# A recommendation tower on one core: ids loads, the split of a product over two steps, the last block's copies, and four products of ones at the start

## The reference

```python
x = layer_norm(dense_t @ Wd.T, gd, bd)                       # 512 x 128
y = layer_norm(jnp.einsum('bnd,ed->bne', sparse_t, Ws), gs, bs)
y = jnp.einsum('bne,pn->bep', y, Wsi)
y = jnp.swapaxes(layer_norm(y, gsi, bsi), 1, 2)              # 512 x 32 x 128
T = jnp.concatenate([x[:, None, :], y], axis=1)              # 512 x 33 x 128
Z = jnp.einsum('bnd,bmd->bnm', T, T)
out = layer_norm(Z[:, TRIL_I, TRIL_J] @ Wl.T, gl, bl) * mask # the first 384 kept
h = jnp.concatenate([out, r_dense_t], axis=1)
h = jnp.maximum(h @ W_top1 + b_top1, 0.0)
h = jnp.maximum(h @ W_top2 + b_top2, 0.0)
y = h @ W_top3
```

## Time and profile before

| | |
|---|---|
| median of 3 executions | 299.44 us (298.72 to 300.36) |
| profiled execution | 297.24 us, span 295.4 us |
| TensorE matmuls busy | 154.6 us, 52% |
| VectorE busy | 130.5 us, 44% |
| ScalarE busy | 107.0 us, 36% |
| GpSimd busy | 100.9 us, 34% |
| granted TensorE clock, whole span | 0.763 |

### The profile page before, as it was taken

One profiled execution on the slowest core, in us unless ns is written; L12 is line 12 of the kernel. 1 busy time (PEld: TensorE's weight loads), 2 busy tenths in 40 slices (PEclk: granted clock), 3 DMA queues, 4 the chain that ended last, 5 costly groups with the idle time before them and its releaser, 6 DMA issues.

```text
span 295.4 us, 4646 instructions
## 1 busy us (share of the span) xinstructions
PE 154.6 (52%) x1819; PEld 116.9 (40%) x1819; DVE 130.5 (44%) x296; ACT 107.0 (36%) x242; POOL 100.9 (34%) x111
## 2 busy tenths in 40 slices
PE   0736400026000400022069797769898998898797
PEld 0514300003000300002015485447776777776696
DVE  4852300000100600000065778458989789978533
ACT  2020100000100100000046766587777767776522
POOL 3777777777777777773000000000000000000100
PEclk9997765555755555555559967579999999999999
DMA  6352231111111111110000000200002000100000
GB/s 192 105 203 63 97 98 25 25 26 27 27 27 27 27 27 27 26 25 18 0 0 3 0 2 0 46 0 2 3 3 46 0 2 2 39 11 23 23 2 0
DMA packets 6259, 9.59 MB, mean 32 GB/s; under 512 B 2687, under 2 KB 3794, under 8 KB 6110
## 3 DMA queue, kind: packets, MB, share of 16 engines
q0 software_dynamic: 3392, 3.45, 6.0%
q1 hardware_dynamic: 2488, 5.08, 5.7%
q10 hardware_dynamic: 358, 0.77, 0.9%
HBM read 8.01 MB, written 0.00 MB: 27 GB/s over the span
## 4 chain that ended last, share of the span: by engine, by line
issue 43%; PE 31%; ACT 13%; DVE 8%; DMA 3%; SPq 1%; ACTq 0%; DVEq 0%
PE psB L307 7%; ACT Zs L595 6%; PE psU L295 4%; PE psG L280 3%; PE psW L338 3%; DVE B L768 2%; ACT U L561 2%; DMA small_sb<-in_small 2%; DVE qA L746 2%; DVE prod L739 2%; PE psH L443 2%; PE psZ L322 2%; ACT sdB L573 2%; PE psW L443 1%; PE psH L452 1%
## 5 line engine op out<-in xcount | busy, mean ns | idle before, releaser
L253 POOL DMA_INDIRECT g_sb<-in_table,row_id x104 | 99.4, 956 | 31.7 <-issue 31.4
L768 DVE TENSOR_TENSOR B<-psB,bias 128x512 f32<-128x512 f32 x32 | 20.8, 687 | 114.2 <-remote 47.5
L307 PE MATMUL psB<-U,ws_g 64*128 64x512 f32 x64 | 21.9, 765 | 63.5 <-issue 52.9
L210 POOL DMA_DIRECT2D Zt<-Zs x2 | 1.1, 552 | 141.4 <-ACT Zs L595 141.4
L295 PE MATMUL psU<-wsi_x,g_sb 128*128 128x192 f32 (+4 forms) x128 | 26.6, 362 | 34.6 <-issue 30.0
L295 PEld LDWEIGHTS psU<-wsi_x,g_sb 128*128 128x128 f32 x128 | 24.1, 232 | 39.4 <-issue 33.3
L595 ACT ACTIVATE Zs<-psZ 32x264 f32<-32x264 f32 x60 | 37.1, 618 | 1.3 <-PE psZ L322 0.2
L567 ACT ACTIVATE sqB<-B 128x512 f32<-128x512 f32 x32 | 19.7, 633 | 43.2 <-DVE B L768 43.2
L307 PEld LDWEIGHTS psB<-U,ws_g 64*128 64x128 f32 x64 | 5.6, 215 | 68.1 <-issue 53.7
L280 PEld LDWEIGHTS psG<-gram,sT 128*128 128x128 f32 x104 | 15.8, 230 | 32.3 <-issue 24.0
L280 PE MATMUL psG<-gram,sT 128*128 128x128 f32 x104 | 19.3, 334 | 17.6 <-issue 17.6
(11 more groups left out here) (132 smaller groups left out, 217.8 us busy)
## 6 DMA issues: line engine op xcount, KB each, us to landing
g_sb<-in_table,row_id POOLq DMA_INDIRECT x104
wl_sb<-in_wl SPq DMA_DIRECT2D x1, 1280.0 KB
w_sb<-in_w SPq DMA_DIRECT2D x2, 512.0 KB
w_sb<-in_w SPq DMA_DIRECT2D x1, 768.0 KB
small_sb<-in_small SPq DMA_DIRECT2D x1, 615.5 KB, 6.4
dense_sb<-in_dense ACTq DMA_DIRECT2D x1, 512.0 KB, 3.6
Zt<-Zs SPq DMA_DIRECT2D x3, 80.0 KB
Zt<-Zs SPq DMA_DIRECT2D x3, 70.0 KB
```

Source lines behind the costliest of these rows:

```text
L253: pool.indirect_dma_start(g_sb[:, k, h * DSP:(h + 1) * DSP], None, table, bass.IndirectOffsetOnAxis(row_id[:, 2 * k + h:2 * k + h + 1], 0) ...
L307: pe.matmul(psB[h][:, :], ws_g[h * DSP:(h + 1) * DSP, :], U[h * DSP:(h + 1) * DSP, u % 2, :], start=True, stop=True).then_inc(B_done, 1)
L768: dve.tensor_tensor(B[:, h, :].rearrange("p (s j) -> p s j", j=PROJ), psB[h][:, :].rearrange("p (s j) -> p s j", j=PROJ), bias[:, :].rearr ...
```

## The change

The ids go to SBUF as one flat tile, so that each of the two loads is one contiguous run in each partition. The second ids load moves behind that of `small_sb` on SP's queue, and ScalarE's queue waits until the first ids have landed before it issues the load of `dense_sb`. TensorE multiplies a matrix of ones by itself four times (128x512 each, into `psU`) before it waits for `small_sb`; the `fills` thresholds of others go from 4 to 5.

`EARLY` goes from 12 to 6. `output(b-1)` moves from ahead of `project` to behind `inner`, and writes `psH` in place of `psW`; VectorE's copy of it moves behind `sums_a`. Waits follow the new places. For the third block (`LAST - 1`) `squares_w` moves behind ScalarE's last DMAs, `layer1` goes ahead of `variance`, and `zT` waits for the product alone. The last output goes to `psB[0]` in place of `psH`.

```diff
-EARLY, ALL = 12, FLIN // P * CW
+EARLY, ALL = 6, FLIN // P * CW
...
-            sp.dma_start(ids_sb[:, :, 0:FIRST_IDS], ids[:, :, 0:FIRST_IDS]).then_inc(d_ids, 16)
-            sp.dma_start(ids_sb[:, :, FIRST_IDS:], ids[:, :, FIRST_IDS:]).then_inc(d_more, 16)
+            sp.dma_start(ids_sb[:, 0:2 * FIRST_IDS], ids[:, 0:2 * FIRST_IDS]).then_inc(d_ids, 16)
             sp.dma_start(small_sb[:, :], small).then_inc(d_small, 16)
+            sp.dma_start(ids_sb[:, 2 * FIRST_IDS:], ids[:, 2 * FIRST_IDS:]).then_inc(d_more, 16)
...
+            act.wait_ge(d_ids, 16)
             act.dma_start(dense_sb[:, :, :], dense).then_inc(d_dense, 16)
...
             def output(b):
                 pe.wait_ge(h2_ready, b + 1)
+                pe.wait_ge(h1_scaled, b + 1)
                 for k in range(K2):
-                    mm = pe.matmul(psW[0:1, FOUT:FOUT + BS], w3_c[:, k:k + 1], h2T[:, k * BS:(k + 1) * BS],
+                    mm = pe.matmul(psH[0:1, FOUT:FOUT + BS], w3_c[:, k:k + 1], h2T[:, k * BS:(k + 1) * BS],
...
+            pe.wait_ge(fills, 4)
+            for n in range(4):
+                pe.matmul(psU[:, :], ones_sb[:, :], ones_sb[:, :].rearrange("p (o e) -> p o e", o=1).broadcast_to([P, 4, P]),
+                          start=True, stop=True)
             pe.wait_ge(d_small, 16)
...
-                if late and j == 0 and b:
-                    output(b - 1)
                 project(t)
...
                 if late and j == 0:
+                    if b:
+                        output(b - 1)
                     linear(b, 0, EARLY)
...
             inner(UNITS - 1)
+            layer1(LAST - 1)
             variance(LAST - 1)
-            layer1(LAST - 1)
             last_block()
...
+                if b == LAST - 1:
+                    act.wait_ge(zT_ready, b + 1)
                 act.activation(z_sq[:, :], psW[:, :], ACT.Square).then_inc(W_squared, 1)
...
-                        squares_w(b)
                     keep_z(t - 1, 1)
...
+            squares_w(LAST - 1)
             deviation_w(LAST - 1)
...
-                dve.wait_ge(W_squared, b + 1)
+                dve.wait_ge(W_squared if b < LAST - 1 else W_done, b + 1)
...
-                if late and j == 0 and b:
-                    copy_y(b - 1)
                 add_b(t, 0)
                 add_b(t, 1)
                 if t + 1 < UNITS:
                     mult_a(t + 1)
                     sums_a(t + 1)
+                if late and j == 0 and b:
+                    copy_y(b - 1)
                 sums_b(t, 0)
```

More of the change, by code:

```diff
@@ L78, in sem @@
             return ctx.enter_context(nc.semaphore(name))
-        ids_sb = sb("ids_sb", [P, 2, 2 * ALL_SLOTS], I32)
+        ids_sb = sb("ids_sb", [P, 4 * ALL_SLOTS], I32)
+        first_ids = ids_sb[:, 0:2 * FIRST_IDS].rearrange("p (a n) -> p a n", a=2)
+        more_ids = ids_sb[:, 2 * FIRST_IDS:].rearrange("p (a n) -> p a n", a=2)
         row_id = sb("row_id", [P, 2 * ALL_SLOTS], I32)
@@ L229, in _ @@
                 if b == 0:
-                    sp.wait_ge(fills, 4)
+                    sp.wait_ge(fills, 5)
                 for q in range(7):
@@ L245, in _ @@
             pool.wait_ge(d_ids, 16)
-            pool.tensor_tensor(row_id[:, 0:FIRST_IDS], ids_sb[:, 0, 0:FIRST_IDS], ids_sb[:, 1, 0:FIRST_IDS],
+            pool.tensor_tensor(row_id[:, 0:FIRST_IDS], first_ids[:, 0, :], first_ids[:, 1, :],
                                ALU.add).then_inc(ids_added, 1)
@@ L331, in linear @@
                     if b:
-                        pe.wait_ge(y_copied, b)
+                        pe.wait_ge(h2_ready, b)
                     else:
@@ L347, in variance @@
                 elif b < LAST - 1:
-                    pe.wait_ge(h1_scaled, b)
+                    pe.wait_ge(y_copied, b)
                 else:
@@ L430, in last_block @@
                 output(LAST - 1)
+                pe.wait_ge(h1s_f[0], 1)
                 for k in range(K2):
                     pe.wait_ge(h2T_f[k], 1)
-                    mm = pe.matmul(psH[0:1, 0:BS], w3_c[:, k:k + 1], h2T_last[:, k * BS:(k + 1) * BS],
+                    mm = pe.matmul(psB[0][0:1, 0:BS], w3_c[:, k:k + 1], h2T_last[:, k * BS:(k + 1) * BS],
                                    start=(k == 0), stop=(k == K2 - 1))
@@ L590, in keep_z @@
                     if b == 0:
-                        act.wait_ge(fills, 4)
+                        act.wait_ge(fills, 5)
                     if b >= 2:
@@ L838, in last_block @@
                 dve.wait_ge(y_done, BLOCKS)
-                dve.tensor_copy(y_sb[:, LAST * BS:], psH[0:1, 0:BS]).then_inc(y_copied, 1)
+                dve.tensor_copy(y_sb[:, LAST * BS:], psB[0][0:1, 0:BS]).then_inc(y_copied, 1)
             def copy_y(b):
@@ L843, in copy_y @@
                 dve.tensor_copy(y_sb[:, b * BS:(b + 1) * BS],
-                                psW[0:1, FOUT:FOUT + BS]).then_inc(y_copied, 1)
+                                psH[0:1, FOUT:FOUT + BS]).then_inc(y_copied, 1)
             dve.memset(eps_c[:, :], EPS).then_inc(eps_ready, 1)
@@ L855, in _ @@
             dve.wait_ge(d_more, 16)
-            dve.tensor_tensor(row_id[:, FIRST_IDS:], ids_sb[:, 0, FIRST_IDS:], ids_sb[:, 1, FIRST_IDS:],
+            dve.tensor_tensor(row_id[:, FIRST_IDS:], more_ids[:, 0, :], more_ids[:, 1, :],
                               ALU.add).then_inc(more_added, 1)
@@ L1043 @@
         "table": np.concatenate(tables, axis=0),
-        "ids": np.stack([chunks(x["ids"]), chunks(np.broadcast_to(starts, (BATCH, NSP)))], axis=1),
+        "ids": np.concatenate([a[:, lo:hi] for lo, hi in ((0, FIRST_IDS), (FIRST_IDS, 2 * ALL_SLOTS))
+                               for a in (chunks(x["ids"]), chunks(np.broadcast_to(starts, (BATCH, NSP))))], axis=1),
         "small": np.concatenate([
```

## The result

The changed kernel takes 300.78 us (median of 20 executions, 298.15 us the fastest), the kernel before in the same comparison 298.61 us (20 executions). The ratio is 1.0077, with a 95% interval of 1.0048 to 1.0105: about 2.3 us slower. A second comparison gave 1.0072 (1.0033 to 1.0111). The medians are over all executions, the ratios over those within about 1.5% of the fastest of their kernel, so a ratio can differ from that of two medians. The profiled execution took 301.19 us with a span of 299.4 us, where before the span was 295.4 us. That is 4.0 us more, nearly twice the median difference, and the reason is in the first part.

What follows compares the result with a forecast made beforehand. Gathers up to the release at 151 us, then each step's loop through ScalarE, were taken as bounds. Terms -1.75 + 2.80 + 0.20 + 0.83 = +2.08 us on the 299.44 us median gave 301.5 us, range 298.2 to 303.7.

Steps and rivals of the forecast that it cites:

- The first gather and the release: Start of the kernel: ids land earlier, so first gather and the release that follows it come 1.75 us earlier.
- the four products of ones cost the path nothing: TensorE's start: products run while it is idle, and everything behind them ends before 151 us in the same lag.
- this cover: The 1.4 us pace of the gathers, hiding a late start of TensorE's records; without it up to 2 us lost.
- The longer product at j = 1: Blocks 0 and 1: 12 more records ahead of the pairwise products make U 1.40 us later each, 2.80 us together.
- The rival of a hidden product: At j = 1 ScalarE waits for VectorE behind sdA anyway, so the 2.80 us go: 298.7 us; chance 0.07.
- j = 0: Two steps: TensorE's relief gives 0.08 us, VectorE's moved copy of y costs 0.28 us; 0.2 us net loss taken.
- Step 15 and the tail: Last step: first copy to `Zs` 1.40 us later, square of 0.57 us off the relays' way; net 0.83 us slower.
- the new wait: Before `last_block`: variance done till about 281.3 us, as the relays land at 281.29 us.
- the rival of the better clock: Steps 4 and 5: `project` quick in both, 1.9 us less, 299.6 us; with L462 298.2 us; chance 0.22.
- The rival that they land no earlier: First ids load: 256 short runs not the only cause, ids gain nothing, 303.3 us; chance 0.15.

Runs made afterwards that it cites:

- the second trace: The changed kernel run again unaltered, on a chip with the lag: 299.96 us against 296.95 us for the kernel before, ratio 1.0072; its profiled execution took 298.26 us.

## Why the prediction was right, and where a step of it failed

The forecast was 301.5 us, with a range of 298.2 to 303.7 and slower as the likeliest; 300.78 us was measured. The ratio of 1.0077 on the 299.44 us that were shown would be 301.7 us. That it fits so well is in part luck: in the profiled execution a miss of 3.5 us at the start and one of 1.5 us in the clock, of opposite sign, stand beside the sum, and the median of the kernel before, from which the forecast starts, was 0.8 us lower in 20 executions than in the three.

*The first gather and the release.* The first gather came 1.88 us earlier for 1.75. That the release follows it held in every trace with the lag: 145.44 us after it here, 146.02 us with the loads alone. The failed step is the one that let "the four products of ones cost the path nothing", with "the release still frees them at once". It took for granted that unit 1's early work is done before the release. In the first trace after it was not: from the release to U(2) are 10.71 us in place of 6.59 us (157.63 minus 151.04), 4.12 us, and they ate the whole gain. I had priced this cover at "up to 2 us". In the second trace it was done, and the gain of 1.64 us was there. The products of ones may be part of the cause. Three of four traces with them and with the lag had U(1) at 144.95 us or later, none of three without them; and EARLY at 12 with the products stood at 0.9995 where the loads alone stood at 0.9943. But that pair also differs in the moved output and the third block's changes, and by the traces the output alone is 0.8 us of the 1.5 us between them. No pair that differs in the products alone ran on a chip with the lag. One sign goes with the late unit 1 in all seven traces with the lag: the first sT on ScalarE stood at 24.52, 29.68 and 32.12 us where it was late, and at 19.52 to 22.14 us where it was not, once with the products. Whether they act, or chance does, stays open. That they are over before L492 needs TensorE was right, and its 16 records took 2.05 us after them, where they had taken 3.13 us; that gain is hidden, as forecast.

*The longer product at j = 1.* 1.40 us a step were forecast, 1.32 us measured in step 7 and in step 11, in both traces, and gone when `EARLY` went back. The rival of a hidden product is out.

*j = 0.* Forecast 0.20 us for the two steps in which the output moves, 10 and 14. Measured were 0.07 us (7.51 against 7.44 us, U(10) to U(11)) and 0.05 us (7.49 against 7.44 us, U(14) to U(15)). The sum is near, but the two parts were both sized too small. TensorE's relief was put at 0.08 us and the move's cost at some 0.2 us; by the experiment with `EARLY` at 12 the move costs 0.40 us, and the relief takes 0.33 us of it back.

*Step 15 and the tail.* Forecast 0.83 us, measured 1.05 and 0.92 us. The first copy to `Zs` moved by 1.47 us counted from U(15) (5.91 against 4.44 us), for 1.40, and ScalarE's relays by 0.95 us (9.84 against 8.89 us); moved alone, the square gave back 0.42 us for 0.57. That the new wait fits "with nothing to spare" was right.

*The clock.* The rival had `project` quick in steps 4 and 5, for 1.9 us. In step 5 it took 1.13 us in both traces after, in step 4 2.08 and 1.28 us. But in step 6 it took 2.08 us in both, where it had taken 1.13 us before. The windows of step 6 (columns as in the earlier trace rows), of the kernel before and of the changed one:

```profile
197.40:205.20 7.80, 7.15 (x110) 5.99 (x110) 5.84 (x13) 5.67 (x14) 0.00 (x0) 1.00 0.01 2
196.29:205.42 9.13, 8.50 (x98) 6.49 (x98) 5.92 (x13) 5.66 (x14) 0.00 (x0) 0.63 0.01 2
```

The granted clock of step 5 rose from 0.55 to 0.83 and that of step 6 fell from 1.00 to 0.63. Step 6 became 1.33 us longer, and steps 3 to 5 together 2.86 us shorter, so that U(2) to U(7) became 1.54 us shorter (0.99 in the second trace). The prediction's ground against the rival, that the same work comes in the same order, did not hold: the low stretch moved. So the rival of the better clock came true by half, beside the forecast and not in place of it. The sum of the second trace without it is +1.99 us, where 2.08 were forecast. In the first the failed step (+3.5 us from forecast) and the clock (-1.5) make up the rest.

*The ids.* The rival that they land no earlier is out, at 1.9 us. The Trainium skill (DMA: Bandwidth & Descriptors, "Queues, rings and completion order") has each DMA engine serve its queues in turn, a packet of each. I took this rule to speak for the rival, since by it ids on SP's queue would not stand behind all of `dense_sb` on ScalarE's. That reading of it was wrong. What the two queues had moved by 3.5 us in the experiment without the hold (q10 carries `dense_sb`, q1 the ids; packets, MB, share of 16 engines):

```profile
q10 hardware_dynamic: 100, 0.41, 31.6%
q1 hardware_dynamic: 69, 0.00, 1.3%
```

Both are served, which agrees with turns. But 100 packets in 0.41 MB are 4 KB each, and those of the ids, one run of 64 bytes in each of 128 partitions, are small. If each turn is one of the trace's packets, 8 KB need nearly as long as 512 KB: 4.1 and 3.9 us, against 1.9 us with those held. This is an argument, not a test of the rule; in the kernel before, q10 had moved 88 packets by 3.0 us and q1 none, and no run tells why.

*What I took for a law.* I read the 1.403 us for each gather as a queue that the program fills. On the other chip the same program shows no such queue, and takes 182.6 us.

## What to carry to other kernels

Where everything waits for one release, ask what each engine will find at that moment: a release that comes 2.4 us earlier is lost if 4 us of one unit's work move behind it. Take work of TensorE that stands ahead of pairwise products or of a square that ScalarE needs at its full price, as soon as the profile shows ScalarE without a wait there. Test edits that stand together one by one: here a move that costs 0.4 us a step was hidden by another edit. And before explaining 0.5% by one trace of each kernel, take a second trace of the same kernel: here two of them differed by 3.0 us in span.

## What the runs showed of the hardware

On some chips, or in some state of them, what TensorE finishes is seen late while GpSimd issues indirect gathers 1.25 us apart: three transposes after 8.40 us, the release 145.2 to 146.1 us after the first gather in seven traces. On another chip the three transposes were seen after 1.62 us. The kernel before takes 297 to 299 us on the former and 182.6 to 182.8 us on the latter. What causes the lag no run here tells. The same edit at a kernel's start was worth 1.7 us on the one kind, and on the other the earlier ids brought unit 0 nothing. And a small load on one queue lands with the large one issued beside it on another queue (4.1 and 3.9 us), unless the large one is held back until it has landed.
